# Attention with the context product one unit later, in one row of small products with the next scores and the transposes

## The reference, cut to what matters

```
h_q = (rmsnorm(x) @ w_q.T).reshape(b, lq, H, DH)
h_k, h_v = the same of the context, with w_k and w_v
score = einsum('bqhd,bkhd->bhqk', h_q, h_k) + position_bias
score = softmax(where(mask, score, -inf))       # over k, in float32
attn = einsum('bhqk,bkhd->bqhd', score, h_v)
out = attn.reshape(b, lq, H * DH) @ w_out.T
x = x + hidden_states + out
```

## Time and profile before

| | us |
|---|---|
| median of 3 runs (lowest, highest) | 832.54 (832.31, 833.41) |
| the profiled execution, its whole time | 832.86 |
| its span, first to last instruction | 831.1 |
| TensorE busy | 825.4 (99%) |
| VectorE busy | 617.8 (74%) |
| ScalarE busy | 392.4 (47%) |
| GpSimd busy | 306.0 (37%) |

### The profile page before, as it was taken

The page is one execution under the profiler, slowest core; times in us unless marked ns, Lnnn a source line. Parts: engine busy times, 40 slices in busy tenths (PEclk is TensorE's granted clock), DMA queues, the critical chain, the costliest instruction groups (busy, mean ns, idle before and its releaser), DMA issues.

```text
span 831.1 us, 12839 instructions
## 1 busy us (share of the span) xinstructions
PE 825.4 (99%) x4330; PEld 698.3 (84%) x4330; DVE 617.8 (74%) x1006; ACT 392.4 (47%) x1009; POOL 306.0 (37%) x279
## 2 busy tenths in 40 slices
PE   9999999999999999999999999999999999999998
PEld 8878888888888878888888888888888888888887
DVE  6867846778776796887778777777767877777765
ACT  6632512432441444544554554554554455456683
POOL 2103211022030044725445445544543544446046
PEclk9999999999999999999999999999999999999999
DMA  8364464673453759414134214314313422423002
GB/s 312 118 228 166 141 218 135 197 253 126 140 179 102 229 162 313 177 57 156 46 117 156 94 69 156 107 56 159 137 52 130 155 87 77 155 78 148 1 1 103
DMA packets 60880, 114.07 MB, mean 137 GB/s; under 512 B 5240, under 2 KB 39160, under 8 KB 55568
## 3 DMA queue, kind: packets, MB, share of 16 engines
q1 hardware_dynamic: 60384, 112.86, 39.6%
q10 hardware_dynamic: 432, 0.39, 0.1%
HBM read 77.58 MB, written 35.65 MB: 136 GB/s over the span
## 4 chain that ended last, share of the span: by engine, by line
PE 98%; DVE 1%; ACT 0%; issue 0%; DVEq 0%
PE out L1356 11%; PE out L1358 11%; PE out L1357 11%; PE proj L1356 10%; PE proj L1358 10%; PE proj L1357 10%; PE o L1474 7%; PE s L1455 7%; PE s L1356 4%; PE s L1358 4%; PE s L1357 4%; PE t L1463 3%; PE proj L1550 1%; PE proj L1551 1%; PE t L1502 1%; PE s L1433 1%
## 5 line engine op out<-in xcount | busy, mean ns | idle before, releaser
L946 ACT ACTIVATE probs<-probs,neg_max 128x128 f32<-128x128 f32 x256 | 99.7, 391 | 132.4 <-DVE neg_max L1201 132.4
L768 POOL TENSOR_TENSOR w_stage<-w_stage 128x256 f32<-128x256 f32 x30 | 27.6, 920 | 305.6 <-DMA w_stage<-in_wk 126.8
L780 POOL TENSOR_TENSOR w_lo<-w_stage,w_hi 128x512 fp32r<-128x512 f32 (+1 forms) x52 | 59.4, 1154 | 140.7 <-ACT w_hi L884 140.7
L1233 DVE TENSOR_TENSOR acc<-out,acc 128x512 f32<-128x512 f32 x100 | 68.4, 688 | 36.8 <-PE out L1358 36.3
L1356 PE MATMUL out<-wo_hi,o_hi 128*128 128x512 f32 x224 | 95.2, 425 | 0.0
L1356 PE MATMUL proj<-x_hi,w_hi 128*128 128x512 f32 x210 | 88.6, 422 | 0.0
L1358 PE MATMUL out<-wo_lo,o_hi 128*128 128x512 f32 x224 | 88.3, 394 | 0.0
L1357 PE MATMUL out<-wo_hi,o_lo 128*128 128x512 f32 x224 | 87.6, 391 | 0.0
L1358 PE MATMUL proj<-x_lo,w_hi 128*128 128x512 f32 x210 | 82.7, 394 | 0.0
L1357 PE MATMUL proj<-x_hi,w_lo 128*128 128x512 f32 x210 | 82.0, 391 | 0.0
L792 POOL TENSOR_TENSOR bias_mask<-bias_raw,mask_neg 128x512 f32<-128x512 f32 x64 | 77.6, 1222 | 10.2 <-DVE probs L1198 10.1
(11 more groups left out here) (363 smaller groups left out, 2137.4 us busy)
## 6 DMA issues: line engine op xcount, KB each, us to landing
k_spill<-ring SPq DMA_DIRECT2D x64, 256.0 KB, 2.8
v_spill<-ring SPq DMA_DIRECT2D x64, 256.0 KB, 2.2
big_stage<-in_wv SPq DMA_DIRECT2D x8, 1024.0 KB, 8.1
w_stage<-in_wq SPq DMA_DIRECT2D x32, 256.0 KB, 4.5
k_first<-k_spill SPq DMA_DIRECT2D x8, 1024.0 KB, 7.4
v_first<-v_spill SPq DMA_DIRECT2D x8, 1024.0 KB, 4.8
wo_raw<-in_wo SPq DMA_DIRECT2D x16, 512.0 KB, 3.3
k_second<-k_spill SPq DMA_DIRECT2D x8, 1024.0 KB, 6.9
```

What stands on the lines that cost most here:

```text
L780: pool.tensor_tensor(lo, staged(m, part), hi.bitcast(F32), ALU.subtract).then_inc(g_wlo, 1)
L946: last = act.activation(probs[:, j % 2, b, :], probs[:, j % 2, b, :], ACT.Exp, bias=neg_max[:, col:col + 1], accum_out=row_sum[:, col:col ...
L1233: dve.tensor_tensor(acc[:, b, :], bank_tensor[:], acc[:, b, :], ALU.add).then_inc(v_acc, 1)
```

## The change

In pairs 1 to 13 a block no longer holds `S` of unit j+1, later `T` of j and later `PV` of j, each between large products. It begins with `PV` of the unit before (j-1), `S` of j+1 and `T` of j in a row, and all items of the block stand behind them. The items of a block stay the same ones in nearly the same order. The normalisation of j+1 stands behind the early items of its block (in C behind all three), and `T` of that unit is the third small product of the next block. The value load `VV` moves into the next pair's first block. No instruction is added or left out.

```diff
+    def together(j, early, late, extra=()):
+        found = [("PV", j - 1), ("S", j + 1), ("EXP", j + 1), ("T", j), ("BM", j + 2)]
+        if bias_of(j + 2) != bias_of(j + 3):
+            found += [("BL", bias_of(j + 2) + 2)]
+        return [*found, *early, ("N", j + 1), *extra, *late]
...
-                      *outs(0, 0), ("N", 4), ("KL", 2), ("VV", 2), *sums, ("PV", 3), *outs(0, 1, 2)]
+                      *outs(0, 0), ("N", 4), ("KL", 2), *sums, *outs(0, 1, 2)]
             continue
         o = p - 1
-        steps += slot(j, outs(o, 3, 4), prod[1], outs(o, 5), [("WX", m, 1)])
-        steps += slot(j + 1, outs(o, 6) + prod[6], outs(o, 7), prod[2] + [("WO", p)], [("WX", m, 2), ("WX", m, 3)])
-        steps += slot(j + 2, prod[5] + prod[7], prod[3], [], [("WOL", p + 1), *load])
-        split_output = [("WO", p + 1)] if 2 * p + 2 == SPLIT else []
-        steps += slot(j + 3, prod[4] + outs(p, 0), outs(p, 1), outs(p, 2), [("KL", p + 2), ("VV", p + 2), *sums, *split_output])
+        final = 2 * p + 2 == SPLIT
+        steps += together(j, outs(o, 3) + prod[1] + outs(o, 4), outs(o, 5), [("VV", p + 1), ("WX", m, 1)])
+        steps += together(j + 1, outs(o, 6) + prod[6] + outs(o, 7), prod[2] + [("WO", p)], [("WX", m, 2), ("WX", m, 3)])
+        steps += together(j + 2, prod[5] + prod[7] + prod[3], [("WOL", p + 1), *load])
+        if final:
+            steps += together(j + 3, prod[4] + outs(p, 0, 1), [("KL", p + 2), *sums, ("WO", p + 1), ("PV", j + 3), ("VV", p + 2), *outs(p, 2)])
+        else:
+            steps += together(j + 3, prod[4] + outs(p, 0, 1), [*outs(p, 2), ("KL", p + 2), *sums])
```

## The result

847.0 us (845.99 to 847.23), against 832.51 of the kernel before, measured with it: 1.0174 times, 95% interval 1.0161 to 1.0186, 14.5 us more. The profiled execution's span is 845.4 us (831.1 before).

A forecast was written before the change was run, and what follows sets the result against it. TensorE, busy for 99% of the span, was taken as the bound. Late transposes of 18.2 us less savings of 1.7 and 0.5 gave +16.0, 848.5 on the median; 847 was taken, around it 843 to 850 us.

The forecast's parts named there:

- C: Short block of three items, normalising unit 4p+3: its transposes come 0.18 us late, 0.24 with their longer group.
- A: Block normalising unit 4p+1: GpSimd's split and bias hold the normalisation; transposes 0.45 us late, 0.51 with their longer group.
- B: Block normalising unit 4p+2: inherits lateness from A and meets GpSimd's splits; transposes 0.59 us late, 0.65 in all.
- D: Block normalising unit 4p, where weights' sums and a bias meet the normalisation: put at 0, upper bound 0.35 us.
- that rival: D too is late by 0.35 us, 4.6 us in all: 851.6 on the forecast of 847; chance 0.16.
- The first rival: In A L1208 gets its turn right behind GpSimd's split, so its transposes are in time: 835.8 us; chance 0.2.
- The sum of the losses: Late transposes in A, B and C: 0.51 + 0.65 + 0.24 us, times 13 pairs, 18.2 us.
- What it saves (2.2): Savings on TensorE: 1.7 us from late context products that go and 0.5 us from fewer borders.
- eight late context products: Context products that waited for the copy of the transposes would go: at most 1.8 us, taken as 1.7.
- two output products: Late for a reason the profile doesn't name; left out of the sum, below 0.8 us together.
- the borders: Some 90 borders from small groups to large products go, 0.01 us each: about 0.5 us saved.
- The worked sum: Losses less savings, +16.0 us: 848.5 us on the median of the kernel before.

The follow-up runs named there:

- experiment 2: Changed kernel with GpSimd adding the next unit's bias ahead of the split of `WX` 1 in block A: 835.65 us, 1.0047 times before.
- experiment 3: Changed kernel without L1207, the product of the reciprocals with the valid rows: 832.0 us, 0.9999 times before.
- experiment 4: Changed kernel with the normalisation ahead of the read of the third item in block C alone: 843.57 us, 1.0138 times before.
- experiments 1: Changed kernel with the normalisation ahead of the third item's read or addition on VectorE in every block: 832.42 us, 1.0007 times before.
- experiment 8: Kernel before with only the context product one unit later, directly ahead of the next scores; transposes and normalisation keep their places: 832.96 us, 1.0007 times before.
- experiment 7: Kernel before with the bias of the next block ahead of the weights' sums in block D: 830.66 us, 0.9978 times before.
- experiment 5: Changed kernel, normalisation one item sooner everywhere; in C, output weights' split behind `OH` and GpSimd's bias ahead of its low half: 828.83 us, 0.9955 times before.

## Why the prediction was right

- **A (0.51 forecast).** 0.46 late and 0.06 longer in pair 6, 0.52; 0.55 on average over the 13 pairs (twelve are 0.45 or 0.50 late, one 0.72). Each link stands in the rows above at its place: split at 6.98, L1217 caught, bias ahead of L1218, end 9.92 (525.55 - 515.63; laid out 9.91). Experiments 2 and 3 show the cause by both of its halves.
- **B (0.65).** Scores to transposes 533.96 - 532.55 = 1.41 for 0.89, and 0.06: 0.58; 0.60 on average. L1217 stands at 7.91 and L1218 ends at 10.54 in the block (laid out 7.88 and 10.56). That more than half of it is inherited is shown by experiment 2.
- **C (0.24).** 0.23 in pair 6, 0.22 on average; experiment 4 took it away, alone.
- **D (0).** Right: no wait, so that rival falls. In pair 6 L1217 is held until the bias is through (546.80), nothing of GpSimd's follows, and L1218 is over at 547.53, 0.77 ahead of its transposes. The first rival (L1208 has its turn behind the split) would have needed L1217 to be through first; experiment 3 is that kernel.
- **The sum of the losses.** 18.2 forecast. Over all 13 pairs the distances between the starts in the trace, beyond the undisturbed ones (0.112 from the last pass of the scores to the transposes, 0.109 within them), come to 17.9.
- **What it saves (2.2) was too small.** 17.9 - 14.3 of the span leaves 3.6. The eight late context products were 1.2 us by the same count (1.7 forecast), the two output products 0.5 (left out), and the borders 0.2 (0.5 forecast). The border is nearly as worked out: a first large product costs 0.314 us and not 0.230, but the last pass ahead of it 0.031 for 0.112, so next to nothing is won by having fewer borders. The rest, 1.7 us, is nearly all a term I didn't have, 1.6 us of it: large products in a long row follow each other a little sooner (below). I had put that at nothing: "that the grouping itself frees more than 0.01 a border is no case" looked at the borders and not at the products between them.
- **The number.** The worked sum was 848.5. That I took 847 was judgement about small differences of large sums and no step; the terms were 0.3 too high in the losses and 1.4 too low in the savings. The mechanism was right; that 847 is met to the digit is luck.
- **What the lay-out hid.** I wrote that the output weights' split in C hides VectorE's delay, and left it at that. It was the next wait in line, about 3 us, and the main reason that experiments 1, 3 and 8 came out above what was expected, by 3.4, 1 and 2 us. By the same lay-out `PT` would start at 5.85 and end 0.58 later, at 6.43, with the product due at 6.36: I could have had it beforehand.

## What to carry to other kernels

Moving a step to an earlier place spends the slack of what it waits for, and the price isn't in the step that moved but in which instructions now meet on the way to it: here four numbers a partition caught behind another engine's instruction, with the next one of that engine directly behind. Lay out one period of all engines in the new order, each link from a row, and set every end against the time at which it is due. Then go on and find what is late next, since undoing the first lays it open. An order that costs 1.7% was worth 0.45% with the same grouping, once the normalisation stood one item sooner and one split behind the step that waited for it.

## What the runs showed of the hardware

- **Who goes next when VectorE and GpSimd hold each other up.** A VectorE instruction of two operands in SBUF that meets one of GpSimd's waits for its end, however small it is (L1217: 0.89 us for 0.17). The others aren't held: in the changed kernel, 361 to 760 us, the reciprocal (L1216) begins 49 times while GpSimd works and always takes 0.17, and the scores' addition (L1208 there), the context's low half (L1225) and the output product's addition (L1243), which read one operand out of TensorE's result, do so 72 times and keep their 0.68 to 0.69. GpSimd's next instruction starts about 0.04 us before the end of the one before (523.85 against 523.89), so it is ahead of a VectorE instruction that depends on the one just released (523.94). One that had been waiting itself goes first (the earlier trace rows and experiment 3). Two dependent VectorE instructions can so be held by two of GpSimd's in a row, one each.
- **Large products in a long row.** Neighbouring large products start 0.2304 us apart on average in the kernel before (6 or 12 in a row; 812 distances between 373 and 731 us, without a row's first one and those with a wait), 0.2301 in experiment 7 (the same rows, next to no waits), 0.2296 in experiment 8 (seven rows of 12 to one of 6, and not the 9 to 12 that I had expected), 0.2290 in the changed kernel and 0.2285 in experiment 5 (18 to 24 in a row). The distances have two levels in the main, 0.226 to 0.227 and 0.231 to 0.236, and those up to 0.228 are 36% before and 69% in experiment 5. Within experiment 5 the gain lies in the later part of the rows: 0.2297 on average up to a row's 12th product, 0.2274 from there on. Over the 1,170 large products of 13 pairs 0.0016 us each are 1.9, and experiments 5 and 7 are 1.8 apart. What sets the level wasn't tried: the other engines' work beside a product differs with its place in the row as well.
- **A weight load that had to wait** makes the next product 0.06 (transposes, 0.167 for 0.109) to 0.10 us (full float32 passes, 0.214 for 0.112) later still, beside the wait itself.
